# Output projections of two chunks moved behind the new state's products, their addition behind the state update

## The reference, cut to what matters

```python
def step(S, inp):
    q_t, k_t, v_t, a_t, b_t = inp
    kS = jnp.einsum('bhd,bhdv->bhv', k_t, S)
    kkS = jnp.einsum('bhd,bhv->bhdv', k_t, kS)
    S = a_t[..., None, None] * (S - b_t[..., None, None] * kkS) + jnp.einsum('bhd,bhv->bhdv', k_t, v_t)
    o_t = jnp.einsum('bhdv,bhd->bhv', S, q_t)
    return (S, o_t)
...
o = _rms_norm(o).astype(x.dtype).reshape(Bx, Tx, H * DV)
return o @ Wo.T
```

## Time and profile before

| what | value |
|---|---|
| median of 3 runs | 7730.36 us (7722.01 to 7734.81) |
| the profiled execution's own time | 7725.71 us |
| its span, first to last instruction | 7723.9 us |
| TensorE products (PE) busy | 6374.1 us, 83% |
| TensorE weight loads (PEld) busy | 4627.0 us, 60% |
| VectorE (DVE) busy | 4577.7 us, 59% |
| ScalarE (ACT) busy | 2620.1 us, 34% |
| GpSimd (POOL) busy | 2256.2 us, 29% |
| mean granted TensorE clock | 0.904 of 2.4 GHz |

### The profile page before, as it was taken

How to read it: one execution, slowest core, us unless ns; L and a number is a source line. 1 busy time by engine, 2 the same in 40 slices (tenths; PEclk the granted TensorE clock), 3 DMA queues, 4 the chain that set the end, 5 groups by cost and what they waited for, 6 DMA issues and landing times. The chain is left out here.

```text
span 7723.9 us, 162627 instructions
## 1 busy us (share of the span) xinstructions
PE 6374.1 (83%) x60192; PEld 4627.0 (60%) x60192; DVE 4577.7 (59%) x9685; ACT 2620.1 (34%) x5275; POOL 2256.2 (29%) x3893
## 2 busy tenths in 40 slices
PE   7888887887888888888888888888888888878886
PEld 4665656656566565656656566565655656566565
DVE  6556575564756646565565755657556475655654
ACT  3224242332423325242242423324233252422421
POOL 2413223141321513214132241413315132241321
PEclk9899898998989989898898989989899898999988
DMA  1100001001010111001100010010101100011100
GB/s 52 31 37 22 26 30 37 28 22 38 20 34 28 30 40 23 22 30 30 40 22 26 30 37 28 22 38 23 31 29 31 40 22 22 31 29 39 22 26 5
DMA packets 376537, 226.37 MB, mean 29 GB/s; under 512 B 336897, under 2 KB 353921, under 8 KB 367489
## 3 DMA queue, kind: packets, MB, share of 16 engines
q1 hardware_dynamic: 375680, 215.29, 9.7%
HBM read 156.54 MB, written 58.72 MB: 28 GB/s over the span
## 5 line engine op out<-in xcount | busy, mean ns | idle before, releaser
L1583 PE MATMUL PS<-BIG 64*64 64x128 f32 (+3 forms) x23200 | 1074.9, 260 | 278.8 <-PEq L2131 96.2
L827 DVE SCALAR_TENSOR_TENSOR PS<-BIG,CW,PS 128x512 f32<-128x512 f32 x1536 | 1156.2, 754 | 197.1 <-DVEq L825 118.8
L1583 PEld LDWEIGHTS PS<-BIG 64*64 64x64 f32 (+2 forms) x23200 | 924.6, 139 | 405.3 <-issue 391.2
L1583 PE MATMUL PS<-XT,BIG 128*128 128x512 f32 x2048 | 1037.3, 639 | 45.9 <-PEq L1894 45.9
L1586 PE MATMUL PS<-CST,BIG 128*128 128x128 f32 x3536 | 613.0, 315 | 431.4 <-PEq L2078 166.8
L1089 POOL TENSOR_TENSOR RSTD<-VAR,NHALF 128x2 f32<-128x2 f32 x202 | 149.3, 739 | 2233.6 <-POOLq L1088 2224.8
L1586 PEld LDWEIGHTS PS<-CST,BIG 128*128 128x128 f32 x3536 | 454.6, 159 | 573.5 <-issue 554.2
L1583 PEld LDWEIGHTS PS<-XT,BIG 128*128 128x128 f32 x2048 | 389.5, 201 | 378.4 <-issue 370.1
L1583 PE MATMUL PS<-BIG,CST 128*128 128x256 f32 (+1 forms) x1360 | 489.9, 504 | 102.0 <-PEq L1964 99.2
L1171 POOL TENSOR_TENSOR BIG<-BIG 128x30 f32<-128x30 f32 (+14 forms) x960 | 494.6, 515 | 136.4
L1168 POOL TENSOR_TENSOR BIG<-BIG 128x30 f32<-128x30 f32 (+14 forms) x960 | 477.4, 497 | 188.5 <-POOLq L1232 64.3
(11 more groups left out here) (152 smaller groups left out, 10194.8 us busy)
## 6 DMA issues: line engine op xcount, KB each, us to landing
BIG<-in_wv SPq DMA_DIRECT2D x16, 2048.0 KB, 7.5
BIG<-in_wo SPq DMA_DIRECT2D x16, 2048.0 KB, 7.6
BIG<-in_wq SPq DMA_DIRECT2D x16, 1024.0 KB, 4.8
BIG<-in_wk SPq DMA_DIRECT2D x16, 1024.0 KB, 7.5
cells_in<-BIG SPq DMA_DIRECT2D x128, 128.0 KB, 2.7
BIG<-cells_in SPq DMA_DIRECT2D x32, 512.0 KB, 3.8
cells_out<-BIG SPq DMA_DIRECT2D x32, 512.0 KB, 3.0
cells_nat<-BIG SPq DMA_DIRECT2D x32, 512.0 KB, 4.2
```

What stands on the lines that cost most here:

```text
L827: op = v.scalar_tensor_tensor(y, pre[:, j:j + G], CW[:, i * TAPS + j:i * TAPS + j + 1], y, ALU.mult, ALU.add)
L1583: return nc.tensor.matmul(out_, l, r, start=start, stop=stop)
```

## The change

On VectorE, in chunks 5 and 6, the addition of the projected tile goes from ahead of the two halves of the state update to behind them. On TensorE, in the same chunks, the wait for bank 2 and the projection go from ahead of the new state's products to behind them; the wait for the addition, which stood behind the new state's products alone, now stands directly behind the projection and still ahead of the transposed keys. The tile of the last chunk and that of the next group's projections stay where they were.

```diff
--- VectorE, recurrence
                     if c == CHUNKS - 1:
                         break
+                    s_update(c, 0)
+                    s_update(c, 1)
                     if c >= 5:
                         projected(c - 5, XS[p])
-                    s_update(c, 0)
-                    s_update(c, 1)
                     keys(c + 1)
--- TensorE, recurrence
-                    if c >= 5:
-                        copied()
-                        projected(c - 5)
                     new_state(c)
...
                     if c >= 5:
+                        copied()
+                        projected(c - 5)
                         added()
                     keys_t(c + 1)
```

## The result

The changed kernel takes 7768.09 us (7764.73 to 7781.0, 4 runs), the kernel before 7726.18 us (7718.63 to 7734.81, 4 runs): the ratio is 1.0057, interval 1.0040 to 1.0074, so slower by 31 to 57 us. A second comparison, with other runs of both, gave 1.0051, interval 1.0037 to 1.0065. Forecast were 11.5 us, 7740, and a range up to 7758.

The account below looks back on a forecast made before the run. VectorE's queue was taken as the bound, through the start of `keys`. +0.36 us in 32 places made 11.5 us: 7737.2 from the profiled 7725.71, 7741.9 from the median; predicted 7740, range 7722 to 7758.

Parts of the forecast that it names:

- The new state first, the update ahead of the addition: Both reorderings: TensorE's new wait keeps 3.9 us of cover and costs nothing; VectorE's 2.15 us state update comes off the chain.
- Sum for one chunk: Sixth chunk's times from the fill's transposes to `keys`: `keys` starts at 905.87 instead of 905.51, +0.36 us.
- 64-to-whole switch: TensorE going from 64-row to whole-array products, new state to projection: starts 0.07 us ahead of modelled end, group 0.10 longer.
- whole-load rival: A whole weight load shows at each switch to whole-array products: +0.54 us a chunk, 17.3 us, 7743.0; chance 0.06.
- 32 x 0.36 = 11.5 us: Whole kernel: the delay of `keys` per chunk times its 32 places, giving 7737.2 from the profiled execution; chance 0.73.
- What counts is therefore one quantity: when VectorE starts `keys`: At the change, TensorE's work between `keys_t` and its wait is covered by 4.17 or 5.11 us, so only that start matters.
- the low clock comes earlier: Clock falls to 1.2 GHz from the new 0.72 us idle ahead of `keys_t`: +1.06 a chunk, 33.9 us, 7759.6; chance 0.10.
- Range and chances: Whole kernel: 7722 to 7758 us; faster 0.10, same 0.70, slower 0.20, with 0.2% (15.5 us) as the bound.
- low clock left out: Clock stays at 2.4 GHz behind the sixth chunk's shortened wait at L1813: 21.1 us come back, 7716.1; chance 0.07.
- TensorE is never late because the state is late: Kernel before: no wait listed for solved updates (L2040) or updated state (L2109); TensorE is late because of VectorE's queue.

Follow-up runs that it names:

- the projection in the wait: Kernel before, with the projection of tiles 0 and 1 behind TensorE's wait for the next chunk's keys, its addition behind VectorE's two normalisations: 7596.45 us, ratio 0.9831.
- the pause: Kernel before, order unchanged, with one more VectorE instruction that nobody reads ahead of the keys of the seventh and eighth chunk: 7747.92 us, ratio 1.0035.
- the product elsewhere: Kernel before, with one more TensorE product behind the solution of the first and of the second chunk, far from the change: 7737.44 us, ratio 1.0014.
- the sixth chunk alone: Kernel before, with the change made in the sixth chunk only and the seventh left as before: 7759.85 us, ratio 1.0044.

## Why the prediction was wrong

*The new state first, the update ahead of the addition*: right. No wait for `u_ready` came up, nothing waits for `s_ready`, and the update's end was never what `keys` waited for.

*Sum for one chunk*: right to 0.01 us in the sixth chunk and to 0.04 in the seventh. Predicted were a wait of 0.72 at L1649, 3.44 at L1813, 4.38 in the seventh chunk, +0.36 on the keys; measured 0.72, 3.44, 4.34, +0.36. (The 10.7 us that it gives as a sign, from the block's start to the keys, is by its own sum 905.87 - 895.28 = 10.59, and 10.59 is what came out.) The 64-to-whole switch with its 0.10 is there: 7.17 us for the projection, from 902.19, 0.07 ahead of the new state's modelled end. The whole-load rival falls with it, and so does the strict reading of the Trainium skill's "TensorE: Matmul & The Clock Gate", section "Part 3: Packing small matmuls — row/col tiling", that a load overlaps products in flight only with other row groups: 6.77 us of loads stand in these 7.17 us of whole-array products.

*"32 x 0.36 = 11.5 us"*: this step failed, and with it "What counts is therefore one quantity: when VectorE starts `keys`". It took the rest of the kernel as fixed, 0 us for the low stretches behind the wait and in the stage ahead, and let the clock in only through two rivals, one where the low level is left out behind the wait, one where it comes ahead of `keys_t`. Neither happened: the clock is 1.00 up to the keys, and the low stretch behind the wait is still there in every sixth chunk, half as long in five of the 16. In their place the low stretch moved by a few us against the work, 10.7 us in the two chunks, and the pattern of low stretches in the stage ahead was lost, 16 us. The rival "the low clock comes earlier" had a price near the measured one, 33.9 us, by a mechanism that the trace refutes. The spread that should have warned me was in the trace of before: the same instructions between the additions of the sixth and seventh chunk took 29.7 to 31.1 us there, and the only difference was where the low clock began.

*Range and chances*: slower by over 0.2% had 0.20, and the range ended 10 us short, since no end of it had the clock in other stages in it. The 0.10 for faster counted in the 0.07 of the low clock left out, though its 7716.1 is only 9.6 us below 7725.71 and so inside the 15.5.

*"TensorE is never late because the state is late"*: right for this order, with no wait at L2109 before or after the change, but not far from its end: with the projection in the wait TensorE waits for the state in 32 places, 36.6 us in all.

What stays open: why the kernel before has fewer low stretches in the stage ahead. 7 and 9 of its 16 groups have at most 27.4 us there; with the change it is 1 and 0, with the pause 0, with the product elsewhere 2, with the sixth chunk alone 3. So each of four small edits ended it, on the chip that ran the second profile of the kernel before as well as elsewhere. That a group's length decides where the next group meets the low stretches is a guess that no run tested, and which lengths would bring the pattern back was not tried.

## What to carry to other kernels

Moving work off a chain gains only if what takes its place is shorter: here the 2.15 us update left the chain, and a round trip of an addition with the next products behind it came in. When TensorE has waits of several us in each pass, put real work into them, as the projection in the wait did, or the clock makes the products behind them dearer. And in such a kernel a change of half a microsecond a pass is not to be multiplied by its count alone: add the spread that equal instruction sequences already show in the trace, in the stages that are not touched too.

## What the runs showed of the hardware that was not expected

Products that nobody reads, laid into two waits a group, made the kernel 43 us faster, and into some more of them 76 us (0.9902). A stage with the same instructions had 29 to 38 us at the low clock in one kernel or another, with nothing changed in it; the kernel before came back at 29.0 after 30.1 in a second profile, the changed one at 36.9 after 37.1. One product more in two chunks, 2.4 us of visible time in all, slowed the kernel by 5 to 18 us.
